# Nearest codes found in two steps: 256 folded pairs on VectorE with a clip on ScalarE, a choice inside the pair afterwards, and all 128 tiles of an image searched in one stage

## The chip, the cores and the metric

One core of a Trainium2 chip runs the whole kernel. The metric is the device time of one execution in microseconds (us), as the median of three runs. A profiled execution has a time of its own: the span from its first to its last instruction.

## What is computed

The input `x` is 8 images of 128 x 128 pixels with 32 channels. Two blocks follow each other, both added to what came in:

```python
x = x + conv_block(gn(x))       # Haar bands, nine small convolutions, attention, inverse Haar
x = x + vq(gn(x), codebook)     # codebook: 512 x 32
# vq, for every pixel:
dists = x_sq - 2.0 * (xf @ codebook.T) + c_sq
vq = codebook[argmin(dists)]
```

`gn` normalises each channel of an image over its pixels. The second line is what the change touches: for each of the 16384 pixels of an image the nearest of 512 codes is found, and that code is added to the pixel. The largest of `2 xf.c - |c|^2` is the smallest distance.

## The kernel before

**Stages.** `body(b, ...)` is run by every engine for b = 0 to 9. Stage b convolves image b (`conv`), searches codes for image v = b - 1 (`quant`), and loads and transposes image b + 1 (`nxt`). Stage 0 has no search, stage 7 loads nothing, stage 8 has the search of the last image and no convolution, and stage 9 only what stage 8 left over. All engines walk the same list `PLAN`, made by `make_plan` on the host, each issuing its own part at each step. So the order on every engine's queue is the order of `PLAN`, and each queue is in order.

**A stage's work on TensorE.** `PLAN` has 120 products in full float32 (`FULL`, two matmul records of 512 columns each) and 318 split terms (one record each). Between them are *turns*, which use the four PSUM banks `score`: 128 `tile` turns (one matmul of 128 pixels by 512 codes; `tile`, L886), 8 `ychunk` turns (four transposes of the image's pixels back to pixel-major order, copied to `ync` by `ycopy` on ScalarE), 8 `xchunk` turns (the same for the next image), and a few small ones: `mean2`, `var2`, `bias2` at the start of the stage and `mean1`, `var1` near its end. `spread_turns` decides between which products a turn goes. It keeps an account of VectorE's time (`ARGMAX` for a tile, `HAAR`, `PASS`) and places the next turn when that account is no more than `SHORT` = 1.17 or `LONG` = 1.38 us ahead of TensorE's. Turns take the banks round robin (`BANK`), so a turn needs the bank of the turn four places before it; `bank_free` is TensorE's wait for that.

**A tile.** TensorE scores it (L886). VectorE takes the eight largest of 512 scores (`maximum`, MAX8, L1499) and then finds the index (`index`, a load of the values and FIND_INDEX8, L1503); the index of tile t is issued behind the maximum of tile t + 1. The bank is free when the index is done (`s_idx`). GpSimd gathers the 128 code rows of 128 bytes by an indirect DMA into `vqc` (`gather`, L1618). After 16 tiles (a chunk) `add` on GpSimd adds the pixels in `ync` (L1632), and SyncE stores `vqc`.

**Late tiles.** `LATE` = 5: tiles 123 to 127 of an image are put off to the start of the following stage, between `mean2` and `bias2`, where the codes scaled for the following image don't exist yet.

**The stage's start.** `statistics`, `mean2`, `var2` on VectorE give the variance, GpSimd the root (`norm`), VectorE the scaled codes `cbs` (`scale_codes`), then `code_parts`, `bias2` and `bias_parts` on ScalarE and VectorE make `cst`, the table that every tile multiplies with. Tile 0 waits for it (`s_parts`).

**ScalarE's other work in its queue.** `evacuate` after each convolution (`z`, L1046), copies of edges behind some of them (`packed_copy`, L1034, six copies behind w12; `edge_copy`, L1023, two copies behind w25, w15, wd1 and wd2), `ycopy` (L1180), `xcopy` and `xorder` (L1169, L1163), `high` and `stack_high` (L1085, L1118: the left operand of the tiles, four casts after tiles 1 and 3 of every eight), `x_squares` (L1146, L1148), `restore`, `weighted_side`, `normal_ll`.

**A tie between two steps at the end of a stage.** `haar` 7 on VectorE follows tile 115, `x_squares(1)` on ScalarE waits for it, then come tiles 116 and 117, `mean1` on VectorE (which waits for the squares) and `var1` on TensorE (which waits for `mean1`).

## Time and profile before

| | |
|---|---|
| runs | 2001.28 us median, 2001.2 to 2004.69 |
| profiled execution, span | 1999.1 us |
| busy share of the span | TensorE 93%, VectorE 88%, GpSimd 63%, ScalarE 51% |
| one full stage | 225.0 us (the same pattern of steps at 708.95 and at 933.97) |
| end of the last convolution | about 1787.4 us |

The table of busy shares is an average over two very different parts: seven stages in which TensorE convolves one image while the others search the one before, and about 210 us at the end in which there is only the search of the last image. A stage's own windows must be read before a share says anything.

### The profile page before, as it was taken

What the parts mean: (1) busy time and instruction counts of PE and PEld (TensorE: products, weight loads), DVE (VectorE), ACT (ScalarE), POOL (GpSimd) and SP (SyncE); (2) the same over time, 40 slices, a digit from 0 to 9 for tenths busy, and PEclk for the clock granted to TensorE, in tenths of its full rate; (3) what the DMA queues carried; (4) which work ended last, traced back from release to release, by engine and by line L of the source; (5) the groups of instructions that cost most, each with busy time, mean ns of one, the idle gap of its engine ahead of it and who ended that gap; (6) DMA issues with size and microseconds to landing.
All of it is one profiled execution on the core that took longest, in us unless ns stands there. A gap on an engine that the chain in (4) does not pass through costs nothing.

```text
span 1999.1 us, 22686 instructions
## 1 busy us (share of the span) xinstructions
PE 1852.8 (93%) x6112; PEld 1114.6 (56%) x6112; DVE 1753.1 (88%) x3923; ACT 1025.9 (51%) x2058; POOL 1259.2 (63%) x1363
## 2 busy tenths in 40 slices
PE   7999999999999999999999999999999999985553
PEld 5654666456754666556754666556754666432221
DVE  5312799999999999999999999999999999989896
ACT  3325464746456464656456464656456453634331
POOL 1001267756777567766777567766677567767876
PEclk8999999999999999999999999999999999995555
DMA  6621463234532463234532463234532463201111
GB/s 190 186 79 48 111 154 99 71 92 117 157 80 69 116 156 104 71 84 128 156 82 70 116 155 104 72 85 128 154 83 54 112 154 90 60 19 34 37 37 32
DMA packets 135024, 197.21 MB, mean 99 GB/s; under 512 B 36977, under 2 KB 82545, under 8 KB 134897
## 3 DMA queue, kind: packets, MB, share of 16 engines
q1 hardware_dynamic: 101808, 178.40, 31.9%
q0 software_dynamic: 32768, 16.84, 5.4%
q8 instruction: 49, 0.80, 0.2%
q14 instruction: 79, 0.64, 0.1%
q10 hardware_dynamic: 320, 0.52, 0.1%
HBM read 117.52 MB, written 23.72 MB: 71 GB/s over the span
## 4 chain that ended last, share of the span: by engine, by line
PE 53%; DVE 29%; POOL 7%; ACT 5%; issue 5%; ACTq 0%; DMA 0%; POOLq 0%; DVEq 0%
PE ring L961 44%; DVE idx L1503 11%; DVE top L1499 10%; PE score L886 6%; POOL vqc L1618 5%; ACT yst L1118 2%; PE score L818 1%; DVE bands L1325 1%; ACT ha L1034 1%; POOL vqc L1632 1%; DVE brs L1388 1%; DVE ha L1388 1%; DVE bands L1443 1%; ACT hb L1034 1%; DVE bands L1439 1%
## 5 line engine op out<-in xcount | busy, mean ns | idle before, releaser
L1618 POOL DMA_INDIRECT vqc<-in_codebook,idx x1024 | 999.8, 976 | 447.9 <-DVE idx L1503 243.5
L1499 DVE MAX8 top<-score 128x8 f32<-128x512 f32 x1024 | 689.1, 683 | 50.1 <-PE score L886 31.3
L1503 DVE FIND_INDEX8 idx<-top,score 128x8 uint32<-128x512 f32 x1024 | 701.9, 689 | 0.0
L886 PE MATMUL score<-cst,yst 98*128 98x512 f32 x1024 | 619.7, 611 | 88.6 <-DVE idx L1503 70.6
L961 PE MATMUL ring<-hfp,wring 128*128 128x512 f32 x2160 | 594.1, 409 | 3.0 <-ACT hfp L1192 3.0
L961 PEld LDWEIGHTS ring<-hfp,wring 128*128 128x128 f32 x2160 | 409.1, 190 | 116.6 <-issue 10.8
L1118 ACT CAST yst<-bands 32x256 fp32r<-32x256 f32 x1024 | 411.7, 402 | 92.2 <-PE score L886 79.9
L961 PE MATMUL ring<-ha,wfull 128*128 128x512 f32 x896 | 439.1, 597 | 5.9 <-POOL ha L1650 5.2
L886 PEld LDWEIGHTS score<-cst,yst 98*128 98x128 f32 x1024 | 204.6, 202 | 293.8 <-DVE idx L1503 175.0
L961 PE MATMUL ring<-hb,wfull 128*128 128x512 f32 x736 | 356.6, 595 | 0.0
L961 PEld LDWEIGHTS ring<-ha,wfull 128*128 128x128 f32 x896 | 168.6, 190 | 150.3 <-issue 126.6
L961 PEld LDWEIGHTS ring<-hb,wfull 128*128 128x128 f32 x736 | 138.5, 189 | 128.3 <-issue 118.3
L1046 ACT ACTIVATE z<-ring,prm 128x512 f32<-128x512 f32 x144 | 98.9, 688 | 192.1 <-PE ring L961 188.0
L1180 ACT COPY ync<-score 128x256 f32<-128x256 f32 x128 | 41.4, 375 | 226.7 <-PE score L818 145.8
L1626 POOL TENSOR_TENSOR yl<-bands,yh 128x256 fp32r<-128x256 f32 x128 | 96.5, 757 | 15.8 <-ACT yh L1085 13.9
L1650 POOL TENSOR_TENSOR ha<-ha,brs 128x512 f32<-128x512 f32 x16 | 17.5, 1118 | 141.2 <-ACT brs L1063 141.0
L961 PE MATMUL ring<-sidep,wring 96*128 96x512 f32 x384 | 103.6, 405 | 0.0
L961 PE MATMUL ring<-pside,wfull 128*128 128x512 f32 x192 | 85.8, 595 | 0.0
L961 PEld LDWEIGHTS ring<-sidep,wring 96*128 96x128 f32 x384 | 72.5, 189 | 20.3
L1632 POOL TENSOR_TENSOR vqc<-vqc,ync 128x512 f32<-128x512 f32 x64 | 82.1, 1283 | 2.8 <-DMA vqc<-in_codebook,idx 1.7
L1606 POOL TENSOR_TENSOR rstd<-veps,power 128x1 f32<-128x1 f32 x16 | 17.4, 1090 | 104.0 <-DVE veps L1467 85.5
L1169 ACT COPY xt<-score 128x512 f32<-128x512 f32 x64 | 37.2, 583 | 80.2 <-PE score L818 57.1
(138 smaller groups left out, 1362.0 us busy)
## 6 DMA issues: line engine op xcount, KB each, us to landing
wring<-wparts SPq DMA_DIRECT2D x119, 384.0 KB, 3.4
hfp<-hfp SPq DMA_DIRECT2D x96, 255.0 KB, 5.1
yst<-yl SPq DMA_DIRECT2D x512, 32.0 KB
vqc<-in_codebook,idx POOLq DMA_INDIRECT x1024
out<-vqc SPq DMA_DIRECT2D x128, 128.0 KB
xnat<-in_x SPq DMA_DIRECT2D x112, 128.0 KB
wfull<-in_weights SPq DMA_DIRECT2D x32, 384.0 KB, 3.6
sidep<-hfp SPq DMA_DIRECT2D x96, 127.5 KB, 3.2
```

The costliest lines, as they stand in the source:

```text
L886: nc.tensor.matmul(score[bank][:, :], yst[0:KST, j % 2, g, wp], cst[0:KST, :], start=True, stop=True).then_inc(s_tile, 1)
L961: t = nc.tensor.matmul(ring[GBANK[key]][:, :, :], w[rows], src[rows], start=(i == first), stop=(i == last))
L1034: t = nc.scalar.copy(tiles[1][to * CH:(to + 1) * CH, dst, PAD:PAD + ROWS], tiles[0][group * CH:(group + 1) * CH, src, PAD + shift:PAD + sh ...
L1046: nc.scalar.activation(z[:, g % 2], bank[:, :, :], ACT.Identity, bias=col("b" + n[1:]))\
L1118: t = nc.scalar.copy(yst[part * CH:(part + 1) * CH, j % 2, g], block_of(par, j, slice(g * CH, (g + 1) * CH)))
L1180: t = nc.scalar.copy(dst[:, j], src[:, j])
L1388: nc.vector.scalar_tensor_tensor(out=dst, in0=z[:, g % 2], scalar=LEAK, in1=z[:, g % 2], op0=ALU.mult, op1=ALU.max).then_inc(s_leaky, 1)
L1499: nc.vector.max(top8[:, t % 4, :], score[bank][:, :]).then_inc(s_top, 1)
L1503: nc.vector.max_index(idx[:, t // CTILES % 2, t % CTILES, :], top8[:, t % 4, :], score[bank][:, :]).then_inc(s_idx, 1)
L1618: nc.gpsimd.indirect_dma_start(vqc[:, c % 2, w * CH:(w + 1) * CH], None, codebook[:, :], bass.IndirectOffsetOnAxis(idx[:, c % 2, k, 0:1], ...
L1626: nc.gpsimd.tensor_tensor(yl[:, j % 2], bands[par][:, :, j].rearrange("p w e i -> p w (e i)"), yh[:, j % 2], ALU.subtract).then_inc(s_yl, 1)
L1632: nc.gpsimd.tensor_tensor(vqc[:, c % 2, :], vqc[:, c % 2, :], ync[:, c % 2, :], ALU.add)\
```

## The change

What it does:

- **Pairs.** Code k and code k + 256 form a pair. The upper half of the score table holds the *difference* of the two codes, so the 512 columns of a tile's score are s(k) and s(k+256) - s(k). ScalarE clips the second half at zero (`rise`, Relu, 128 x 256, into `best`); VectorE adds the first half and takes the maximum in one instruction (`tensor_tensor_reduce`), then finds the index among 256. A bank is free after that first instruction (`s_top`), no longer after the index.
- **Inside the pair.** Rows of a table `pairs` in device memory hold both codes, their scaled difference and a threshold, 97 values (388 bytes). The scaled part is made once per stage: `table` on TensorE (two small matmuls), `table_rows` on ScalarE, two DMAs on SyncE. The gather fetches such a row. Every eight tiles `select` on VectorE runs four dependent instructions (multiply, reduce, compare, copy where upper), and `add` on GpSimd now covers eight tiles instead of sixteen.
- **Output.** The sum is written to `ync` and stored from there; `ycopy` waits for the store two chunks back instead of for `add`.
- **No late tiles.** `LATE` = 0; all 128 tiles lie in their own stage. `ARGMAX` is 1.2 instead of 1.286.
- **Space.** `pside` now lies over `sidep`, so SyncE's side copies wait for the last product of the stage before, and GpSimd writes the zero borders anew each stage (`rims`, `shore`).

```diff
-LATE = 5
+LATE = 0
-ARGMAX = 1.286
+ARGMAX = 1.2
...
+BOUNDARY = [("mean2", 6.9), ("var2", 9.3), ("scale2", 13.5), ("bias2", 16.9), ("table", 17.6)]
...
             def store(v, c):
-                sp.wait_ge(s_add, PRIMED + XCHUNKS * v + c + 1)
+                sp.wait_ge(s_add, HALVES * v + 2 * c + 2)
...
+            def table(v):
+                sp.wait_ge(s_tabs, v + 1)
+                wait(sp, s_add, HALVES * (v - 1))
+                for i in range(2):
+                    sp.dma_start(pairs[v % 2][i * P:(i + 1) * P, 2 * CH:ROW], tabs[:, i, :]).then_inc(s_table, 16)
...
                     if what == "tile" and 1 <= b <= IMAGES:
-                        return pe.wait_ge(s_idx, TILES * (b - 1) + k + 1)
+                        return pe.wait_ge(s_top, TILES * (b - 1) + k + 1)
...
+            def table_rows(v):
+                act.wait_ge(s_tabled, v + 1)
+                wait(act, s_table, 32 * v)
+                src = score[BANK["table",]][:, 0:2 * P].rearrange("p (i n) -> p i n", i=2)
+                nc.scalar.copy(tabs[:, :, :], src[:, :, 0:CH + 1]).then_inc(s_tabs, 1)
+
+            def rise(v, t, bank):
+                n = TILES * v + t
+                act.wait_ge(s_tile, n + 1)
+                wait(act, s_idx, n + 1 - SLOTS_R)
+                nc.scalar.activation(best[:, n % SLOTS_R, :], score[bank][:, PAIRS:CODES], ACT.Relu)\
+                    .then_inc(s_rise, 1)
...
             def ycopy(v, c):
                 act.wait_ge(s_yT, XCHUNKS * v + c + 1)
-                wait(act, s_add, PRIMED + XCHUNKS * v + c - 1)
+                wait(act, s_store[c % 2], 32 * ((XCHUNKS // 2) * v + c // 2))
...
             def maximum(v, t, bank):
-                wait(dve, s_tile, TILES * v + t + 1)
-                nc.vector.max(top8[:, t % 4, :], score[bank][:, :]).then_inc(s_top, 1)
+                dve.wait_ge(s_rise, n + 1)
+                nc.vector.tensor_tensor_reduce(
+                    out=best[:, n % SLOTS_R, :], in0=score[bank][:, 0:PAIRS], in1=best[:, n % SLOTS_R, :], scale=1.0,
+                    scalar=-ABSENT, op0=ALU.add, op1=ALU.max, accum_out=top8[:, t % 4, 0:1]).then_inc(s_top, 1)
...
+            def select(v, q):
+                n, c, h = HALVES * v + q, q // 2, q % 2
+                rows = picked[:, n % SLOTS_G, :].rearrange("p (t e) -> p t e", e=ROW)
+                y = ync[:, c % 2, h * JTILES * CH:(h + 1) * JTILES * CH].rearrange("p (t e) -> p t e", e=CH)
+                dve.wait_ge(s_yev, XCHUNKS * v + c + 1)
+                dve.wait_ge(s_gather[n % SLOTS_G], 128 * (n // SLOTS_G + 1))
+                after(nc.vector.tensor_tensor(prod[:, :, :], rows[:, :, 2 * CH:3 * CH], y, ALU.mult), s_lean, 3 * n + 1)
+                after(nc.vector.tensor_reduce(lean[:, 0, :], prod[:, :, :], AXIS.X, ALU.add), s_lean, 3 * n + 2)
+                after(nc.vector.tensor_tensor(lean[:, 1, :], lean[:, 0, :], rows[:, :, 3 * CH], ALU.is_gt),
+                      s_lean, 3 * n + 3)
+                upper = lean[:, 1, :].bitcast(U32).rearrange("p (t o) -> p t o", o=1).to_broadcast([P, JTILES, CH])
+                nc.vector.copy_predicated(rows[:, :, 0:CH], upper, rows[:, :, CH:2 * CH]).then_inc(s_select, 1)
...
                 nc.gpsimd.indirect_dma_start(
-                    vqc[:, c % 2, w * CH:(w + 1) * CH], None, codebook[:, :],
-                    bass.IndirectOffsetOnAxis(idx[:, c % 2, k, 0:1], 0)).then_inc(s_gather[c % 2], 16)
+                    picked[:, n % SLOTS_G, w * ROW:(w + 1) * ROW], None, pairs[v % 2][:, :],
+                    bass.IndirectOffsetOnAxis(idx[:, c % 2, k, 0:1], 0)).then_inc(s_gather[n % SLOTS_G], 16)
```

## Rows read from the trace of the kernel before

**Rows 1.** The page: busy time of the engines over the span

```profile
PE 1852.8 (93%) x6112; PEld 1114.6 (56%) x6112; DVE 1753.1 (88%) x3923; ACT 1025.9 (51%) x2058; POOL 1259.2 (63%) x1363
```

**Rows 2.** Busy time by window: one full stage, and the search alone

```profile
core 0: us, PE busy (x) PEld busy (x) DVE busy (x) ACT busy (x) POOL busy (x), PEclk, DMA share, GB/s
709.00:934.00 225.00, 221.69 (x762) 136.25 (x760) 217.37 (x487) 127.98 (x260) 156.91 (x165) 1.00 0.41 107
...
1809.00:1992.00 183.00, 99.73 (x156) 39.89 (x154) 163.55 (x385) 57.74 (x148) 141.96 (x151) 0.50 0.16 35
```

**Rows 3.** The chain of work, start and us: split terms, then full records

```profile
745.96 3.10 PE ring L961 x13
...
792.81 4.33 PE ring L961 x10
```

**Rows 4.** TensorE in order of time: the first tile of a stage, and its wait

```profile
909.58 0.60 PE L818 MATMUL score<-idn,bands 128*128 128x128 f32 x4
911.89 0.47 PE L886 MATMUL score<-cst,yst 98*128 98x512 f32 x1 [1.71 <-issue]
```

**Rows 5.** GpSimd in order of time: gathers in the search alone, an add

```profile
1872.99 1.28 POOL L1632 TENSOR_TENSOR vqc<-vqc,ync 128x512 f32<-128x512 f32 x1
1874.43 0.96 POOL L1618 DMA_INDIRECT vqc<-in_codebook,idx  x1 [0.16 <-issue]
...
1886.33 0.94 POOL L1618 DMA_INDIRECT vqc<-in_codebook,idx  x1 [0.31 <-issue]
1887.58 0.95 POOL L1618 DMA_INDIRECT vqc<-in_codebook,idx  x1 [0.30 <-issue]
...
1895.42 1.27 POOL L1632 TENSOR_TENSOR vqc<-vqc,ync 128x512 f32<-128x512 f32 x1
```

**Rows 6.** Groups by line and shape: count, busy us, mean ns, idle before

```profile
L1618 POOL DMA_INDIRECT vqc<-in_codebook,idx x1024 | 999.8, 976 | 447.9 <-DVE idx L1503 243.5 <-issue 195.4 <-DMA out<-vqc 7.8
L1503 DVE FIND_INDEX8 idx<-top,score 128x8 uint32<-128x512 f32 x1024 | 701.9, 689 | 0.0
L1499 DVE MAX8 top<-score 128x8 f32<-128x512 f32 x1024 | 689.1, 683 | 50.1 <-PE score L886 31.3 <-POOL vqc L1632 17.4
L1118 ACT CAST yst<-bands 32x256 fp32r<-32x256 f32 x1024 | 411.7, 402 | 92.2 <-PE score L886 79.9
L1180 ACT COPY ync<-score 128x256 f32<-128x256 f32 x128 | 41.4, 375 | 226.7 <-PE score L818 145.8 <-POOL vqc L1632 80.0
L1321 DVE TENSOR_TENSOR sd<-xt 128x256 f32<-128x256 f32 x56 | 23.4, 417 | 0.0
L1626 POOL TENSOR_TENSOR yl<-bands,yh 128x256 fp32r<-128x256 f32 x128 | 96.5, 757 | 15.8 <-ACT yh L1085 13.9
```

**Rows 7.** ScalarE in order of time: from the end of w12 on

```profile
708.36 0.69 ACT L1046 ACTIVATE z<-ring,prm 128x512 f32<-128x512 f32 x1 [0.76 <-PE ring L961]
708.95 4.05 ACT L1034 COPY ha<-ha 32x960 f32<-32x960 f32 x4
713.02 2.03 ACT L1034 COPY hb<-hb 32x960 f32<-32x960 f32 x2
715.08 0.65 ACT L1180 COPY ync<-score 128x256 f32<-128x256 f32 x2
```

**Rows 8.** TensorE in order of time: tile 19, the fourth turn behind the y transposes

```profile
715.77 0.50 PE L886 MATMUL score<-cst,yst 98*128 98x512 f32 x1
```

**Rows 9.** ScalarE in order of time: from the end of w25 to past wd1

```profile
801.35 0.69 ACT L1046 ACTIVATE z<-ring,prm 128x512 f32<-128x512 f32 x1 [4.05 <-PE ring L961]
804.03 2.03 ACT L1023 COPY hb<-hb 64x960 f32<-64x960 f32 x2 [1.99 <-DVE hb L1401]
...
815.89 2.03 ACT L1023 COPY ha<-ha 64x960 f32<-64x960 f32 x2 [1.18 <-DVE ha L1388]
...
819.62 3.30 ACT L1118 CAST yst<-bands 32x256 fp32r<-32x256 f32 x8
```

**Rows 10.** VectorE in order of time: the last step of mean1

```profile
876.10 0.22 DVE L1284 SCALAR_TENSOR_TENSOR vsum<-dev,vx 128x1 f32<-128x1 f32 x1
```

More of the change, by code:

```diff
@@ L10 @@
 U32 = mybir.dt.uint32
+AXIS = mybir.AxisListType
 P = 128
@@ L173 @@
 STARTS, SPREAD = bank_turns()
-TURNS = [x for x, _ in STARTS if x[0] not in ("var2", "scale2")] + SPREAD
+ORDERED = [x for x, _ in STARTS] + SPREAD
+TURNS = [x for x in ORDERED if x[0] not in ("var2", "scale2", "var1")]
 assert len(TURNS) % BANKS == 0
@@ L177 @@
 BANK["var2",] = BANK["mean2",]
+BANK["var1",] = BANK["mean1",]
 HAAR_AT = {c * CTILES + (XTURN if c < XCHUNKS - 1 else LASTX) + XDELAY - 1: c for c in range(XCHUNKS)}
-RUN_ENDS = [x[1] for x, y in zip(TURNS, TURNS[1:] + [("end",)]) if x[0] in ("tile", "late")
+RUN_ENDS = [x[1] for x, y in zip(ORDERED, ORDERED[1:] + [("end",)]) if x[0] in ("tile", "late")
             and (x[1] in (*HAAR_AT, NORMAL_AT, MAIN_TILES - 1, TILES - 1) or y[0] in ("mean1", "var1"))]
@@ L460, in conv_vq_kernel @@
         wparts = nc.dram_tensor("wparts", [P, NP * PAGE_SLOTS, P], F32, kind="Internal").ap()
+        pairs = [nc.dram_tensor(f"pairs{i}", [PAIRS, ROW], F32, kind="Internal").ap() for i in range(2)]
         at = (nc.sbuf_base + 31) // 32 * 32
@@ L710, in _ @@
                 sp.dma_start(dst[:, :], src[:, :]).then_inc(s_const, 16)
+            for rows in pairs:
+                for h in range(2):
+                    sp.dma_start(rows[:, h * CH:(h + 1) * CH], codebook[h * PAIRS:(h + 1) * PAIRS, :])\
+                        .then_inc(s_static, 16)
             def stack(v, j):
@@ L777, in body @@
                         stack(v, 1)
+                    elif quant and what == "table":
+                        table(v)
                     elif quant and what == "tile":
@@ L828, in bank_free @@
                         return pe.wait_ge(s_xev, XCHUNKS * (b + 1) + k + 1)
-                    if what in ("mean1", "var1") and b <= IMAGES - 2:
-                        return pe.wait_ge((s_dev if what == "mean1" else s_veps)[0], b + 2)
+                    if what == "mean1" and b <= IMAGES - 2:
+                        return pe.wait_ge(s_veps[0], b + 2)
                     if what == "ychunk" and 1 <= b <= IMAGES:
@@ L986, in body @@
                         bias2(v)
+                    elif quant and what == "table":
+                        bank_free(b, step)
+                        table(v)
                     elif quant and what == "ychunk":
@@ L1224, in body @@
                         bias_parts(v)
+                    elif quant and what == "table":
+                        table_rows(v)
+                    elif v > 0 and what == "late":
+                        rise(v - 1, step[1], BANK[step])
                     elif quant and what == "tile":
+                        rise(v, step[1], BANK[step])
                         j, k = step[1] // JTILES, step[1] % JTILES
@@ L1529, in body @@
                         pending = n, t, bank
+                        if t % JTILES == 4 and t > JTILES:
+                            select(n, t // JTILES - 1)
+                        if what == "tile" and t == 2 and n:
+                            select(n - 1, HALVES - 1)
                         if t in RUN_ENDS:
@@ L1673, in body @@
                             pending = None
-                        if t % CTILES == 11 and t > CTILES:
-                            add(n, t // CTILES - 1)
-                        if t == 3 and v:
-                            add(v - 1, XCHUNKS - 1)
+                        if t % JTILES == 6 and t > JTILES:
+                            add(n, t // JTILES - 1)
+                        if what == "tile" and t == 5 and n:
+                            add(n - 1, HALVES - 1)
                     elif nxt and what == "var1":
                         norm(0, b + 1)
+                    elif conv and what == "edge" and step[1] == 0:
+                        shore(b)
                     elif conv and what == "mm":
```

138 lines of the change are left out of this document (96 added, 42 removed).

## The prediction

> **What bounds the kernel now.** I read the busy table first, and distrust it: TensorE 93% and VectorE 88% [rows 1] look like two engines at their limit, and the change takes work from VectorE alone. The table by windows separates the parts. In a full stage of 225.0 us TensorE is busy 221.7 and VectorE 217.4 us, ScalarE only 128.0; in the search alone at the end TensorE's clock is at 0.50 (1.2 GHz, where it was at 1.00, or 2.4 GHz, in the stage), and VectorE and GpSimd share the time [rows 2].
>
> How much of the 225.0 us TensorE really needs is worked out from its own durations. Thirteen split terms took 3.10 us, so 0.2385 each; ten full records took 4.33 us, so a full product (two records) costs 0.87 us [rows 3]. A stage has 120 products (104.4 us), 318 terms (75.8), 128 tiles at 0.235 (30.1; the step from tile to next matmul in the stage, about one split term), 16 groups of transposes at 0.44 (7.0) and about 1.1 for the small ones: 218.4 us. So **TensorE stands idle 6.6 us per stage**, and that is all that a faster VectorE could give back there. Walking the program's order of turns with these costs and setting it against the times at which the tiles ran shows where it goes: about 3.2 us at the stage's start, where tile 0 waits for the code table (1.7 us of it as one wait [rows 4]), and 3.4 us in three places where VectorE or GpSimd was late.
>
> In the search alone the bound is neither TensorE nor VectorE. The gathers follow each other every 1.25 us (0.95 busy and 0.30 with nothing awaited), and from one add to the next 22.43 us pass for 16 tiles, with GpSimd nearly never waiting for an index [rows 5]. VectorE's pair of MAX8 and index steps every 1.26 us there (0.69 + 0.68 us overlapped, [rows 6]) but then stops for GpSimd.
>
> **VectorE's saving.** Before, 683 + 689 ns of searching per tile over 512 columns, in a step of 1.26 us [rows 6]. What 256 columns cost on VectorE has a row of another kind: a two-input pass of 128x256 takes 417 ns [rows 6], so I take 0.42 each for the sum with maximum and for the search, in all about 0.85 us per tile with the load of the values. The bounds are 0.75 (both halved in full) and 1.3 (nothing gained). `select` adds per eight tiles three passes of 256 elements and a tiny one with a semaphore between each: 3 x 0.42 + 0.15 + 0.15 = 1.5 us, 24 us per stage. VectorE's stage: 217 - 128 x 1.26 + 128 x 0.85 + 24 = 189 us (176 to 247). It stops being near the bound, unless nothing is gained per column. All this lies beside TensorE, so it brings at most the 3.4 us per stage.
>
> **What goes to ScalarE.** The clip reads 128x256 from PSUM as `ycopy` does: 375 ns, and two of those take 0.65 us [rows 6, 7]; I take 0.33 per tile, bounds 0.28 and 0.40. 128 of them are 42 us: ScalarE goes from 128 to 170 of 225 us, 76%. That sum looks harmless. But the clip is put into a queue in order, between a tile's matmul and the instruction that frees its bank. Before, a long block on ScalarE delayed the y and x copies alone; now it delays every tile behind it, and TensorE stops when four turns are outstanding. So each block is set against the turns that the changed plan places behind it:
>
> (a) *Behind w12.* From the start of w12's last evacuation to the end of the y copy behind six packed copies, 7.4 us pass (708.36 to 715.73) [rows 7]. In the plan before, the fourth turn behind the y transposes (tile 19) came 7.5 us after that product and ran at 715.77, just as its bank came free [rows 8]. In the changed plan the transposes come 1.7 us and tile 19 5.5 us after it: 1.9 us stall. Then ScalarE does clip, cast, clip, four casts (1.65 us, half of a 3.30 row [rows 9]) and clip before tile 18's bank is free: some 0.7 us more. 2.6 us.
>
> (b) *Behind w25, wd1 and wd2.* The evacuation of w25 starts, and 4.7 us later the edge copies are done (801.35 to 806.06), since ScalarE waits for VectorE in between; behind wd1 the edge copies and the squares together hold it from 815.89 to 819.62 [rows 9]. Behind each there is a y copy or `x_squares`, then tiles 0 to 3 of an eight with their four casts twice. Following the queue from w25's end on: tile 83 waits 0.15, tile 85 0.75, tile 92 0.95, tiles 100 and 101 0.85 each: 3.5 us.
>
> (c) *Behind haar 7.* `x_squares(1)` waits for VectorE's haar after tile 115. Before, tiles 116 and 117 were searched on VectorE while ScalarE squared. Now their clips wait behind the squares (1.7 us, from 817.92 to 819.62 [rows 9]), so `mean1`, which is behind their searches, ends some 8.6 us after tile 115's matmul. Before it was about the same (876.32 [rows 10], tile 115 at 867.9), but `var1` had a place 9.8 us after that matmul in the plan and now has one 6.3 us after it. 2.3 to 3.2 us, taken as 2.8.
>
> Sum 8.9 us of new stalls, against 3.4 us of old ones that go: **+5.5 us in a full stage**, 33 us in six. In stage 7 there is no next image, so (c) and the x copies are away; (a) and half of (b) remain, against 3.4: +1 us. Stage 0 has no search. Bounds: if ScalarE never makes TensorE wait the 3.4 us come back, -20 us over six stages; with 0.40 per clip and each stall half as long again it is +60.
>
> On exactly this the Trainium skill ("ScalarE: Activation LUTs", Rules for kernel authors) says for `relu`: use VectorE, not ScalarE. Here the clip as a pass on VectorE would cost another 0.42 by the row above, 54 us per stage, for 243 in 225; by that sum the rule doesn't fit a stage in which VectorE is at 217, yet what it warns of, ScalarE as the wrong place, is what my sum finds through the queue.
>
> **The stage's start.** The late tiles leave it: 5 x 0.235 = 1.2 us less TensorE work before tile 0 (they come back later in the stage, so nothing in sum), and VectorE is 2.5 us earlier with the scaled codes. But ScalarE is busy with eight casts until after that and then makes the table in a chain; tile 0 becomes possible about 1 us earlier, and TensorE arrives 1.1 us earlier. The 3.2 us stay. `table` adds two small matmuls (0.2 us; by the nearest rows between 0.06 and 0.9), a copy on ScalarE (0.35) and two DMAs on SyncE. Behind SyncE's wait for them are page loads, four pages ahead, which bear 2 us. Behind GpSimd's wait for the table is gather 0, some 1 to 2 us later. Zeroing of borders on GpSimd is ten short memsets, under 2 us, on an engine with slack in the stage (128 x 1.25 + 30 = 190 of 225). The side copies that now wait for the last product started just after it anyway. I cost these at nothing in the stage; cover gone would be 1 to 2 us.
>
> **The end.** GpSimd per 16 tiles: 16 x 1.25 = 20.0, two `low` passes at 0.61 more than the gap they fill (1.2), and the add: 1.15 more before, now two halves of 128x256. The row for that size on GpSimd is 757 ns [rows 6], so again 0.61 each beyond the gap, 1.2. 22.4 before, 22.5 after. The tiles that a faster VectorE delivers earlier find GpSimd at its own pace. The first gather comes about 0.7 us later, early waits for VectorE (some 4 us) mostly go, and at the very end stands `select` (+1.5) and a shorter add (-0.5). Sum for the end: -1 us, -4 to +3.
>
> **Sum.** 33 + 1 - 1 = +33 us on the profiled 1999.1 us, whose run lies as its span plus about 2.2 at the median of 2001.3: **2034 us**.
>
> **Rivals.**
> 1. *ScalarE keeps up.* Shares speak for it (76% busy), and the plan has gaps of 3 us behind each haar in which it catches up. Then TensorE's 3.4 us per stage come back: 2001.3 - 20 - 1 = 1980 us. Against it: block (a) passed before with no margin [rows 7, 8]. Chance 0.22, with a spread of 1975 to 1997.
> 2. *Both cancel*, stalls of 3.4 us per stage: 2001 us, within 4. Chance 0.08.
> 3. *The gather becomes dearer.* A row has 388 bytes instead of 128. If GpSimd needs 0.3 us more per gather (its unexplained 0.30 again), 128 x 1.55 + 30 = 228 us per stage make it the bound, and the end grows by 128 x 0.3 = 38 us: 2001 + 7 x 6 + 38 = 2081 us. It decides from about 0.25 us more per gather. For it: GpSimd alone sets the end [rows 5]. Against it: the number of rows per gather is unchanged at 128. Chance 0.08. The Trainium skill ("DMA: Bandwidth & Descriptors", Bandwidth) calls transfers below 64 KB descriptor-dominated, which would leave a gather of 50 KB near one of 16 KB.
> 4. *VectorE gains nothing*: the new pair costs 1.25 per tile, stage 217 + 24 = 241: 2001 + 7 x 16 + 15 = 2128 us. Chance 0.04.
>
> My forecast with its own range of 2005 to 2060 has 0.58: slower, at 2034. The range for 8 in 10 leaves out the far end of rival 1 and rivals 3 and 4: 1980 to 2058. Faster by over 0.2% (what a measurement of this kernel can tell from no change) 0.22, same 0.08, slower 0.70.
>
> **What would show it.** Steps right: stages of about 230.5 us; waits of TensorE's tiles and y/x turns for VectorE's new maximum or ScalarE's y copy, clustered behind w12, wd1, wd2 and before `var1`; ScalarE near 170 us busy per stage and VectorE near 190; gathers every 1.25 us and 22.5 us per 16 tiles at the end. Wrong: a stage of 221 to 222 us (rival 1), gathers further apart than 1.25 us in the end (rival 3), or a VectorE step per tile above 1.1 us (rival 4). The weakest step is (b), a queue followed over 40 us in which each delay shifts what comes behind it.

## The result: 213 us slower, and the profile after

The changed kernel takes 2214.7 us (median of four runs, 2214.0 to 2223.1), the kernel before 2001.2 us beside it: a ratio of 1.108, 95% interval 1.106 to 1.110. The forecast was slower, at 2034 us; the measured time lies far above its range. The profiled execution has a span of 2212.7 us. The experiments below are one execution each, so their times carry the scatter of single runs (the kernel before beside them: 1998.4 to 2002.2 us).

The page's line of busy times, which answers to [rows 1]:

```profile
PE 1920.9 (87%) x6144; PEld 1134.3 (51%) x6144; DVE 1422.7 (64%) x5465; ACT 1340.8 (61%) x3090; POOL 1283.7 (58%) x1483
```

The groups by line and shape that answer to [rows 6] (line, engine, operation, shapes, count, busy us, mean ns, idle time before them and what ended it):

```profile
L1725 POOL DMA_INDIRECT picked<-pairs,idx x1024 | 1002.7, 979 | 561.5 <-DVE idx L1579 360.4 <-issue 183.4 <-DMA pairs<-tabs 16.9
L1579 DVE FIND_INDEX8 idx<-top,best 128x8 uint32<-128x256 f32 x1024 | 424.9, 419 | 0.0
L1572 DVE CUSTOM_DVE_ANT_0 best<-score,best 128x256 f32<-128x256 f32 x1024 | 418.0, 415 | 469.5 <-ACT best L1175 467.1
L1175 ACT ACTIVATE best<-score 128x256 f32<-128x256 f32 x1024 | 365.6, 380 | 390.7 <-DVE idx L1579 284.6 <-PE score L931 100.9 <-issue 2.0
L1579 DVE MATCH_VALUE_LOAD idx<-top,best 128x8 f32 x1024 | 86.4, 84 | 1.7
L1572 DVE DVE_READ_ACCUMULATOR2_ANT top<- 128x1 f32 x1024 | 85.2, 83 | 0.0
L1589 DVE TENSOR_TENSOR prod<-picked,ync 128x256 f32<-128x256 f32 x128 | 55.8, 436 | 51.1 <-DMA picked<-pairs,idx 50.8
```

Every price was about as forecast: VectorE's fold 415 ns and its search 419 ns, the clip 380 ns, the gather 979 ns where it was 976 [rows 6]. VectorE is busy 330 us less than before [rows 1], and yet no engine is above 87%. The lines of the fold (L1572) and of the clip (L1175) say why: before each fold VectorE stood idle for ScalarE's clip, 467.1 us in all, and before each clip ScalarE stood idle for VectorE's index, 284.6 us. Each of the two engines waits for the other (e3 below tells what the second of these waits is worth).

Busy time by window (us, then each engine's busy time, the granted clock, the DMA share, GB/s), for one full stage from `mean2` to `mean2` and for the search alone at the end, against [rows 2]:

```profile
734.33:990.25 255.92, 231.96 (x765) 138.28 (x764) 175.74 (x679) 166.77 (x387) 160.23 (x180) 0.97 0.43 111
1999.00:2212.00 213.00, 100.63 (x171) 44.02 (x170) 137.41 (x599) 107.56 (x296) 147.41 (x162) 0.51 0.23 51
```

This stage takes 255.9 us where it took 225.0. The last convolution ends at 1999.3 us (before at 1787.4, of a span of 1999.1), so the search alone behind it takes 213.4 us, 1.6 more than before. Everything else, some 212 us, came in the stages: 194 in the six full ones (from tile 0 to tile 0, 32 each) and 18 in stage 7.

### The profile page after: what moved, and what is told of

Read it like the earlier page. It is cut to its first block, busy times and chain, and to the rows that moved or that the text cites. A ratio compares the mean times of both kernels' runs of the same rounds, so it can differ in the third digit from the quotient of the medians.

```text
span 2212.7 us, 26665 instructions
## 1 busy us (share of the span) xinstructions
PE 1920.9 (87%) x6144; PEld 1134.3 (51%) x6144; DVE 1422.7 (64%) x5465; ACT 1340.8 (61%) x3090; POOL 1283.7 (58%) x1483
## 4 chain that ended last, share of the span: by engine, by line
PE 34%; DVE 24%; ACT 15%; issue 12%; DMA 8%; SPq 4%; POOL 3%; ACTq 0%; DVEq 0%; POOLq 0%
PE ring L1008 30%; DVE idx L1579 6%; ACT yst L1185 6%; DVE best L1572 4%; DMA xnat<-in_x 4%; DMA picked<-pairs,idx 4%; ACT best L1175 3%; PE score L931 3%; POOL picked L1725 2%; DVE picked L1594 2%; DVE lean L1590 2%; DVE prod L1589 2%; DVE ha L1461 1%; SPq L754 1%; SPq L777 1%
## 5 line engine op out<-in xcount | busy, mean ns | idle before, releaser
L1725 POOL DMA_INDIRECT picked<-pairs,idx x1024 | 1002.7, 979 | 561.5 <-DVE idx L1579 360.4
L1572 DVE CUSTOM_DVE_ANT_0 best<-score,best 128x256 f32<-128x256 f32 x1024 | 418.0, 415 | 469.5 <-ACT best L1175 467.1
L1175 ACT ACTIVATE best<-score 128x256 f32<-128x256 f32 x1024 | 365.6, 380 | 390.7 <-DVE idx L1579 284.6
L1008 PE MATMUL ring<-ha,wfull 128*128 128x512 f32 x896 | 461.8, 622 | 29.9 <-DVE ha L1461 29.3
L1579 DVE FIND_INDEX8 idx<-top,best 128x8 uint32<-128x256 f32 x1024 | 424.9, 419 | 0.0
L1008 PE MATMUL ring<-hb,wfull 128*128 128x512 f32 x736 | 368.1, 615 | 9.1 <-DVE hb L1474 5.7
L1742 POOL TENSOR_TENSOR ync<-ync,picked 128x256 f32<-128x256 f32 x128 | 101.1, 790 | 5.6 <-DVE picked L1594 3.3
L1589 DVE TENSOR_TENSOR prod<-picked,ync 128x256 f32<-128x256 f32 x128 | 55.8, 436 | 51.1 <-DMA picked<-pairs,idx 50.8
L1579 DVE MATCH_VALUE_LOAD idx<-top,best 128x8 f32 x1024 | 86.4, 84 | 1.7
L1572 DVE DVE_READ_ACCUMULATOR2_ANT top<- 128x1 f32 x1024 | 85.2, 83 | 0.0
```

The costliest lines, as they stand in the source:

```text
L1008: t = nc.tensor.matmul(ring[GBANK[key]][:, :, :], w[rows], src[rows], start=(i == first), stop=(i == last))
L1175: nc.scalar.activation(best[:, n % SLOTS_R, :], score[bank][:, PAIRS:CODES], ACT.Relu)\
L1572: nc.vector.tensor_tensor_reduce(out=best[:, n % SLOTS_R, :], in0=score[bank][:, 0:PAIRS], in1=best[:, n % SLOTS_R, :], scale=1.0, scalar= ...
L1579: nc.vector.max_index(idx[:, t // CTILES % 2, t % CTILES, :], top8[:, t % 4, :], best[:, n % SLOTS_R, :]).then_inc(s_idx, 1)
L1589: after(nc.vector.tensor_tensor(prod[:, :, :], rows[:, :, 2 * CH:3 * CH], y, ALU.mult), s_lean, 3 * n + 1)
L1725: nc.gpsimd.indirect_dma_start(picked[:, n % SLOTS_G, w * ROW:(w + 1) * ROW], None, pairs[v % 2][:, :], bass.IndirectOffsetOnAxis(idx[:, c ...
```

## Where a stage loses its time

As for the forecast, I set the tiles' times against the program's order of turns. TensorE loses 37.5 us per stage to waits and to a lower clock behind them, where it lost 6.6. By place: the stage's start 2.8; behind w12 3.0; tiles 30 to 74 6.3; tiles 80 to 101 (w25, wd1, wd2) 13.2; from `mean1` to tile 121 9.2; in pieces under 0.6 us 3.0.

The largest single piece is at wd2's start. The changed kernel in order of time (start, us, operation, idle time before it and its releaser), first TensorE:

```profile
890.18 1.02 PE L1008 MATMUL ring<-hb,wfull 128*128 128x512 f32 x2
895.72 2.05 PE L1008 MATMUL ring<-ha,wfull 128*128 128x512 f32 x2 [4.51 <-DVE ha L1461]
```

ScalarE in the same stretch:

```profile
888.35 0.71 ACT L1230 COPY xord<-xnat 128x256 f32<-128x256 f32 x2 [1.26 <-DMA xnat<-in_x]
888.96 0.65 ACT L1175 ACTIVATE best<-score 128x256 f32<-128x256 f32 x2
889.50 0.69 ACT L1096 ACTIVATE z<-ring,prm 128x512 f32<-128x512 f32 x1
890.30 0.38 ACT L1175 ACTIVATE best<-score 128x256 f32<-128x256 f32 x1
892.50 0.38 ACT L1175 ACTIVATE best<-score 128x256 f32<-128x256 f32 x1 [1.81 <-DVE idx L1579]
892.78 0.68 ACT L1096 ACTIVATE z<-ring,prm 128x512 f32<-128x512 f32 x1
897.70 2.02 ACT L1073 COPY ha<-ha 64x960 f32<-64x960 f32 x2 [4.23 <-DVE ha L1461]
```

And VectorE:

```profile
889.37 0.42 DVE L1572 CUSTOM_DVE_ANT_0 best<-score,best 128x256 f32<-128x256 f32 x1 [3.21 <-ACT best L1175]
...
890.13 0.40 DVE L1589 TENSOR_TENSOR prod<-picked,ync 128x256 f32<-128x256 f32 x1
...
891.23 0.47 DVE L1594 COPY_PREDICATED picked<-lean,picked 128x256 f32<-128x256 uint32 x1
...
892.91 0.41 DVE L1393 TENSOR_TENSOR sd<-xt 128x256 f32<-128x256 f32 x1
...
894.36 1.21 DVE L1461 SCALAR_TENSOR_TENSOR ha<-z 128x512 f32<-128x512 f32 x1
```

Read it as one story. ScalarE waits 1.26 us for an x transfer that has nothing to do with the search. Behind that copy stand two clips, so VectorE stands for 3.21 us, though the haar's input behind its fold had been ready since 887.08 (`xt`, copied by ScalarE). When the clip comes, VectorE does fold, index, `select` (890.13 to 891.70), a fold and two searches, a haar (892.9 to 894.4) and only then the leaky step of wd1, whose input z had been ready at 890.2: 4.2 us late. TensorE, which needs that `ha`, stands 4.51 us. Meanwhile ScalarE stands 1.81 us for an index three tiles back and then 4.23 us for the second half of that `ha`, which VectorE makes behind two more folds and two searches (896.99 to 897.67). Behind ScalarE's edge copies and the squares of `x` the next clips wait: VectorE stands again, 4.15 us before its fold at 901.81. A delay on either queue is handed to the other and comes back.

Before, VectorE's searches waited only for TensorE (31.3 us in all) and for GpSimd (17.4) [rows 6]; none of them waited for ScalarE.

## The experiments

Two parts of the diff stand apart in most of them: the clip, and ARGMAX 1.2, which places tiles, y transposes, `mean1` and `var1` closer (1.286 is the constant of the kernel before).

**e1, no clip on ScalarE.**

```diff
-                        rise(v, step[1], BANK[step])
...
-                dve.wait_ge(s_rise, n + 1)
+                dve.wait_ge(s_tile, n + 1)
+                wait(dve, s_idx, n + 1 - SLOTS_R)
                 nc.vector.tensor_tensor_reduce(
-                    out=best[:, n % SLOTS_R, :], in0=score[bank][:, 0:PAIRS], in1=best[:, n % SLOTS_R, :], scale=1.0,
+                    out=best[:, n % SLOTS_R, :], in0=score[bank][:, 0:PAIRS], in1=cb4[:, 0:PAIRS], scale=1.0,
```

> The kernel after without the clip on ScalarE: the first pass of VectorE adds a constant table from SBUF instead of the clipped second half, so the choice of code is not the reference's. ScalarE is out of the tile's path, all else (select, table, gathers of 388 bytes, spacing) stays. Theory (the clip's place in ScalarE's queue, between the matmul and the instruction that frees the bank, makes the time): stages fall from 255.9 to 220 to 228 us, time 1975 to 2025 us. Rival 1 (select and the gathers it waits for on VectorE make the time): stages stay above 240, time above 2110. Rival 2 (the new spacing with all 128 tiles in one stage makes it): stages stay above 240 as well.

2077.7 us: 137 us come back, but 76 more than before remain, 53 above the expected band. So the clip's place in the queue is the largest part, and something that I had costed at nothing makes up the rest. A stage took 234.6 us, with TensorE's losses spread: start 2.8, tile 19 2.2, tile 64 1.7, tile 83 1.3, `mean1` 1.6, `var1` 2.5, tiles 119 to 121 2.6.

**e2, ScalarE as busy, but nobody waits.** VectorE folds as in e1.

```diff
-SLOTS_G, SLOTS_R = 3, 3
+SLOTS_G, SLOTS_R = 2, 3
...
-                wait(act, s_idx, n + 1 - SLOTS_R)
-                nc.scalar.activation(best[:, n % SLOTS_R, :], score[bank][:, PAIRS:CODES], ACT.Relu)\
-                    .then_inc(s_rise, 1)
+                wait(act, s_rise, n)
+                nc.scalar.activation(spare[:, :], cb4[:, 0:PAIRS], ACT.Relu).then_inc(s_rise, 1)
```

> As the run without the clip, but ScalarE runs a Relu of 128x256 per tile at the clip's place on data in SBUF, after the tile's matmul; nobody waits for it (the choice of code is not the reference's; two gather slots instead of three make room). If ScalarE's occupied time alone delays its evacuations: 2080 to 2200 us. If it is the wait of VectorE and of the bank for the clip that costs: within 25 us of the run without the clip.

2113.7 us, 36 above e1 and 101 below the changed kernel: in the first band, and 11 above the second. The stand-in reads SBUF and takes 417 ns where the clip takes 380, so it fills 53 us of ScalarE's time per stage and the clip 46. That time costs some 36 us in the whole run; what is left of the clip, above all that VectorE and the bank wait for it, costs the other 101. The two gather slots are a second difference between these kernels; in e11 below they come with six slots for the clip and cost nothing.

**e3, six slots in place of three**, so that ScalarE may clip further ahead:

```diff
-SLOTS_G, SLOTS_R = 3, 3
+SLOTS_G, SLOTS_R = 2, 6
```

> Complete kernel, six buffers for the clipped scores instead of three (two gather slots instead of three), so ScalarE never waits for VectorE's index of three tiles before. In the profile after, ScalarE idles 285 us on that wait. Theory that this wait closes a circle (VectorE stops in select or haar, ScalarE stops for it, and y copies and evacuations queue behind): 2100 to 2170 us. If the wait is only where ScalarE would have been idle anyway: within 15 us of 2214.

2191.7 us, 23 less, outside both bands. ScalarE's wait for the index is gone (2.8 us in all, before the edit 284.6), but it then waits for TensorE's tile:

```profile
L1175 ACT ACTIVATE best<-score 128x256 f32<-128x256 f32 x1024 | 361.8, 381 | 301.3 <-PE score L931 294.5 <-DVE idx L1579 2.8 <-issue 1.1
```

VectorE still stands 430.4 us for the clip, where it stood 467.1. So the distance of three tiles is a small part: a late clip is late however far it was allowed ahead. If delays come back to ScalarE at a high price, then by its other waits for VectorE, those of the edge copies and squares for the leaky and haar steps. That way was seen in the rows above; no run took it out.

**e4, `select` left out:**

```diff
-                after(nc.vector.tensor_tensor(prod[:, :, :], rows[:, :, 2 * CH:3 * CH], y, ALU.mult), s_lean, 3 * n + 1)
...
-                nc.vector.copy_predicated(rows[:, :, 0:CH], upper, rows[:, :, CH:2 * CH]).then_inc(s_select, 1)
+                nc.vector.memset(lean[:, 0, :], 0.0).then_inc(s_select, 1)
```

> The kernel after with the four instructions of select left out (the wait for the gathers and for the y copy stays, a small memset signals; the lower code of every pair is always taken). Theory of the clip's place: VectorE is not the bound, 10 to 60 us less than 2214. Rival (select is the cause): below 2100.

2139.5 us, 75 less: more than the 10 to 60 that I gave it, though not the rival's 115. The forecast had put `select` on VectorE as 24 us a stage "beside TensorE". It was not beside: the four instructions stood between late clips and late leaky steps. `select`'s wait for the gathers stays in this kernel (89.7 us of VectorE's idle time), so the 75 us are the price of the four instructions alone.

**e5 to e7, the spacing.** The first line is e5; e6 adds e1's edit; e7 adds the others to e5, the clip as a pass on VectorE with none on ScalarE:

```diff
-ARGMAX = 1.2
+ARGMAX = 1.286
...
+                dve.wait_ge(s_tile, n + 1)
+                nc.vector.tensor_scalar_max(best[:, n % SLOTS_R, :], score[bank][:, PAIRS:CODES], 0.0).then_inc(s_rise, 1)
                 dve.wait_ge(s_rise, n + 1)
```

> Complete kernel after with ARGMAX = 1.286 as before, so the turns lie further apart again (tile 19 comes 7.9 us behind w12's last product instead of 5.7, var1 9.8 us behind tile 115 instead of 6.3). Theory (the spacing is a cause of its own beside the clip): 2140 to 2185 us. If only the clip's place counts: within 15 us of 2214.

> ARGMAX = 1.286 and no clip on ScalarE (VectorE adds a constant table, the choice of code is not the reference's). The run without the clip took 2078 us with the tight spacing; its idle time of TensorE sat at tile 19, at mean1 and var1 and at tiles 64 and 83. Theory: tile 19, mean1 and var1 pass again, 2010 to 2045 us. Rival (select and its gathers make the rest): above 2060 us.

> Complete kernel, ARGMAX = 1.286, the clip as a pass of its own on VectorE (128x256, 0.42 us, 54 us per stage on top of some 171 busy). Theory (the place of the clip costs more than its length): faster than the same spacing with the clip on ScalarE, 2070 to 2140 us. If VectorE's length decides: over 2180 us.

2142.3, 2014.6 and 2131.3 us, all as expected. The spacing is worth 72 us with the clip and 63 without it: the two parts nearly add. In the plan for 1.2 the first y transposes behind w12 come 1.7 us after its end and `var1` some 6.3 us after tile 115; in that for 1.286 it is 4.0 and 9.8 us, by the forecast's prices. The clip on VectorE, as the Trainium skill ("ScalarE: Activation LUTs", Rules for kernel authors) has it for `relu`, is 11 us better than on ScalarE here. The runs agree with that rule, though by little, and both lie 130 to 141 us above the kernel before: a third pass per tile costs on either engine.

**e8, e11, e12: two mends, together and apart.** e11 gives e5 the slots of e3. e12 moves `select` and the add one tile later, so that the gathers' transfers have landed. e8 does both:

```diff
-                        if t % JTILES == 4 and t > JTILES:
+                        if t % JTILES == 5 and t > JTILES:
                             select(n, t // JTILES - 1)
...
-                        if t % JTILES == 6 and t > JTILES:
+                        if t % JTILES == 7 and t > JTILES:
                             add(n, t // JTILES - 1)
```

> Complete kernel with the clip on ScalarE, ARGMAX = 1.286, six buffers for the clipped scores (two gather slots), and select and add one tile later each. Theory: the parts add up, 2100 to 2160 us; still slower than before, since evacuations stay behind the clips in ScalarE's queue.

> ARGMAX 1.286 with SLOTS_G, SLOTS_R = 2, 6 (complete kernel): ScalarE may clip six tiles ahead of VectorE's index in place of three, and the gathers have two slots in place of three. Beside the next run this tells which of e8's two edits made it 27 us slower than e5 (2142.3). At ARGMAX 1.2 the same edit gained 23 us: if it gains here too 2115 to 2135; if two gather slots are too few at this spacing, over 2150 with GpSimd's adds late and TensorE's clock lower than e5's 0.935.

> ARGMAX 1.286 with select one tile later (fifth tile of an eight in place of the fourth) and the add one tile later. Expected if select's wait for the gathers' transfers is what holds VectorE: 2125 to 2140. If it is this edit that cost e8 its 27 us: 2150 to 2175, since the y copy behind it then waits for the store of a later add.

2169.2, 2141.8 and 2184.5 us, in the order e8, e11, e12: all three outside their bands. At this spacing the slots do nothing beside the early `select` (e11 against e5) and gain 15 us beside the late one (e8 against e12). The later `select` costs 42 us, though its wait for the gathers fell (0.8 us between 700 and 956 us of the trace, in e5 1.6). I expected a gain for e8, and it was 27 us worse than e5.

The traces show where: over the six full stages e12 loses 50 us between tiles 102 and 115 and e5 13, and in five of them 4.55 us go before tile 106 alone. GpSimd there adds `brs` to `ha` and to `hb`, two sums at a time. e12, GpSimd:

```profile
918.19 2.15 POOL L1771 TENSOR_TENSOR ha<-ha,brs 128x512 f32<-128x512 f32 x2
...
923.50 2.15 POOL L1771 TENSOR_TENSOR hb<-hb,brs 128x512 f32<-128x512 f32 x2
```

VectorE, and TensorE behind it:

```profile
918.21 2.42 DVE L1589 TENSOR_TENSOR prod<-picked,ync 128x256 f32<-128x256 f32 x1
...
923.05 2.90 DVE L1397 TENSOR_TENSOR bands<-sd 128x256 f32<-128x256 f32 x1
```

```profile
926.68 0.50 PE L931 MATMUL score<-cst,yst 98*128 98x512 f32 x1 [3.98 <-DVE top L1572]
```

`select`'s multiply and a haar pass, usually 0.4 us each, took 2.42 and 2.90, and each ended 0.3 us behind GpSimd's pair. In e5 one haar pass stands beside the first pair (1.69 us), and beside the second only folds and searches, which took no longer than usual. So one tile later puts two of VectorE's passes beside GpSimd's sums instead of one. That the sums hold VectorE is read from the times; no run moved them.

**e9, TensorE kept busy in two of its waits.** The windows around wd2's start (columns as above) show the granted clock beside TensorE's idle time:

```profile
885.00:890.00 5.00, 4.94 (x13) 2.42 (x14) 1.78 (x12) 3.68 (x10) 2.93 (x4) 1.00 0.48 137
890.00:895.00 5.00, 1.21 (x4) 0.33 (x2) 4.86 (x17) 1.53 (x4) 2.94 (x4) 0.82 0.19 46
895.00:900.00 5.00, 4.28 (x6) 2.16 (x7) 2.66 (x10) 2.27 (x3) 3.02 (x3) 0.50 0.39 81
900.00:905.00 5.00, 5.00 (x15) 2.60 (x15) 2.09 (x11) 4.93 (x15) 1.00 (x2) 1.00 0.07 19
```

TensorE was busy 1.21 of 5 us, and the clock fell from 1.00 (2.4 GHz) to 0.50 (1.2 GHz) until 900 us. The step of a product with its tile was 2.27 and 2.09 us behind the wait, 1.10 before it. The kernel before has no such stretch: from 250 us to its last convolution the clock is at 1.00 in every window of 2.5 us. Over the stages (250 us to the last convolution) TensorE is busy 1587 us here and 1512 before, and some 48 of these 75 us are the lower clock (busy time in windows of 2.5 us, times one less the clock). That looked like a cause of its own, so e9 fills two waits with matmuls that nothing reads:

```diff
+            def fill(dst, times):
+                for _ in range(times):
+                    nc.tensor.matmul(dst, cst[0:KST, 0:P], cst[0:KST, CODES - dst.shape[-1]:CODES], start=True, stop=True)
...
+                    if b > 0 and (n, half) == ("wd2", 0) and i == first:
+                        for _ in range(17):
+                            nc.tensor.matmul(ring[GBANK[key]][:, :, :], cst[0:KST, 0:P], cst[0:KST, :],
+                                             start=True, stop=True)
                     inputs_ready(b, n, half, m, kind, low)
...
                         bank_free(b, step)
+                        if quant:
+                            fill(score[BANK[step]][:, PAIRS:CODES], 20)
                         mean(0, b + 1, BANK[step])
```

> The changed kernel with matmuls that nothing reads, put in front of two of TensorE's long waits: 20 of 98x128 by 98x256 before mean1's (its wait was 2.85 us), 17 of 98x128 by 98x512 into wd2's own bank before its first input (4.51 us); the next start=True overwrites them. TensorE waits as long but isn't idle. In the changed kernel's trace the granted clock was at 0.50 behind these two places (895 to 900 and 950 to 956 us) and at 1.00 ahead of them, and never below 1.00 in a stage of the kernel before. Theory 'the idle time costs twice, once as a wait and once as half the clock behind it': the clock stays at 1.00 behind wd2's start and mean1, and since a product with its tile took 2.1 us there and 1.09 at full clock, 2.2 us and up to 3 us a stage come back: 2214.7 less 15 to 35 us, 2180 to 2200. Rival 'TensorE would wait for VectorE there anyway, so its clock is free': within 6 us of 2214.7, at a clock of 1.00 or not. Slower by more than 6 us if the fillers run on beyond the wait.

2223.1 us: not 15 to 35 less, but 8 more, as long as the slowest of the changed kernel's own four runs. TensorE of e9 in order of time:

```profile
892.85 4.43 PE L1010 MATMUL ring<-cst 98*128 98x512 f32 x17
898.45 1.13 PE L1017 MATMUL ring<-ha,wfull 128*128 128x512 f32 x2 [1.17 <-DVE ha L1472]
...
905.12 0.50 PE L936 MATMUL score<-cst,yst 98*128 98x512 f32 x1 [1.15 <-DVE top L1583]
```

And the window of e9 behind the fillers:

```profile
897.50:902.50 5.00, 4.05 (x12) 2.19 (x12) 2.98 (x10) 1.97 (x2) 3.31 (x4) 1.00 0.34 72
```

At wd2's start the edit did what it should: the clock stayed at 1.00 and the step was 1.1 to 1.2 us. But TensorE then met VectorE's fold 1.15 us too early, and from the product behind the wait to `mean1` it took 52.55 us (898.45 to 951.00), in the changed kernel 52.53 (895.72 to 948.25). What the clock gave was handed back as waits: there the lower clock is a symptom, and the pace is set by VectorE and ScalarE. At `mean1` the edit worked by half: its wait fell from 2.85 to 0.37 us, but `var1` then waited 3.79 us where it had waited 2.39, and behind it the clock fell all the same (0.52 from 955 to 960 us). The fillers ran on beyond neither wait (1.17 and 0.37 us of idle time behind them). By the sum above 31 us of lower clock were left of the 48.

**e10, e2's edit at 1.286.**

> ARGMAX 1.286, and ScalarE does its clip on other data in SBUF that nobody waits for (VectorE folds with a constant, so the second half of the scores is left out of the search): the queue is as long, the handshake is gone. At this spacing the clip with its handshake cost 128 us (2142.3 against 2014.6). Theory 'the handshake is the larger part': 2030 to 2060. Rival 'ScalarE's queue is the larger part': over 2080. At ARGMAX 1.2 the occupancy alone was worth 36 us.

2052.0 us, as expected: 37 above e6 and 90 below e5. ScalarE's time costs the same at both spacings (36 and 37), and the wait nearly so (101 and 90).

**e13, e14, e17: the length of ScalarE's blocks.** From the second image on the edge copies move one column:

```diff
+                width[0] = 1 if b else ROWS
...
-                    t = nc.scalar.copy(tiles[1][p, dst, PAD:PAD + ROWS], tiles[0][p, src, PAD:PAD + ROWS])
+                    t = nc.scalar.copy(tiles[1][p, dst, PAD:PAD + width[0]], tiles[0][p, src, PAD:PAD + width[0]])
```

(and so for line 1084), in the changed kernel (e13), in the kernel before (e14), and in e1 (e17).

> The changed kernel, but from the second image on the 14 edge copies of a stage on ScalarE (lines 1073 and 1084, 1.00 us each) move one column in place of 64, so the edges are old ones; their waits for VectorE and their signals stay. About 12 us of ScalarE's 167 go, all of it out of the long blocks that the prediction named in (a) and (b). Theory 'it is the blocks': behind them the clips come late, and most of the 101 us that the clip's handshake costs (2214.7 against e2's 2113.7) goes with them: 2110 to 2155. Rival 'it is the handshake at every tile, and the waits of the blocks, not their copies': 2180 to 2210.

> The control: the same edit in the kernel before (lines 1023 and 1034 there; from the second image on the edges are old ones). TensorE stands idle some 3.4 us a stage there outside the stage's start, and the copies lie ahead of a few x and y turns: 1985 to 2001. A gain of more than 20 us would mean that e13's gain is not the clip's.

> e13's edit without the clip: ARGMAX 1.2, no clip on ScalarE (the second half of the scores is left out of the search), and the edge copies of one column from the second image on (old edges). With the clip the short copies gained 66 us, in the kernel before 14. Theory 'their length matters through the clip's queue': 2055 to 2070 against e1's 2077.7. Rival 'they gain as much at this spacing without the clip': 2010 to 2030.

2148.6, 1986.5 and 2047.1 us: 66, 14 and 31 us less, the first two as expected. The same microseconds of ScalarE cost nearly five times as much with the change as before. Without the clip half of the gain is left (e17 missed both bands, in the middle). What makes the copies count twice as much as before even there, the closer places or something else of the change, wasn't tried apart.

**e15, e16: `select` with and without the clip, at 1.286.**

> ARGMAX 1.286 and select's four instructions left out (a memset in their place, so the lower code of each pair is always taken). At ARGMAX 1.2 select cost 75 us, of which 24 a stage of VectorE's time were not on any path by the prediction. Theory 'select holds VectorE's queue, and the clip's handshake passes that on whatever the spacing': 2060 to 2090. Rival 'select mattered at 1.2 because the tiles came too close': 2115 to 2140.

> e15's edit without the clip: ARGMAX 1.286, no clip on ScalarE (VectorE folds with a constant, so the second half of the scores is left out of the search), and select's four instructions left out. With the clip select cost 60 us at this spacing (2142.3 against 2082.3). Theory 'the handshake makes VectorE's queue a part of TensorE's way': without it select costs little, 1998 to 2010 against e6's 2014.6. Rival 'select costs the same by itself': 1950 to 1975, which would lie below what TensorE needs.

2082.3 and 1997.1 us (the latter 1 us below its band). Without `select` the time falls by 60 us with the clip, by 17.5 without it. This shows the coupling most plainly: VectorE's queue matters three times as much once the clip ties ScalarE to it. Both kernels keep `select`'s wait for the gathers, 104 us of VectorE's idle time in e16, which is as fast as the kernel before: that wait is no part of the loss.

Put in a row, each step is one measured difference:

| kernel | us | step |
|---|---|---|
| before, beside e16 | 1998.4 | |
| e16: all but clip, `select` and spacing | 1997.1 | -1 |
| e6: with `select` | 2014.6 | +17 |
| e10: with the clip's time on ScalarE | 2052.0 | +37 |
| e5: with the wait for the clip | 2142.3 | +90 |
| the change: with ARGMAX 1.2 | 2214.7 | +72 |

e10's two gather slots are inside its two steps. Another order of the steps would give other sizes, since they act on each other (`select` is 17 us without the clip and 60 with it). No version here beats the kernel before: only the incomplete e14 and e16 lie below it.

## Why the prediction was right and where it failed

*Right.* The direction. VectorE's price: I took 0.85 us per tile; two folds followed each other at 884.58 and 885.33, so 0.75, the lower bound. The clip's 0.33 (two took 0.63 us), ScalarE's 170 us per stage (166.8), `select`'s 1.5 us (1.57). The gather's price, and with it the end:

```profile
2120.74 0.69 POOL L1742 TENSOR_TENSOR ync<-ync,picked 128x256 f32<-128x256 f32 x1
...
2124.11 0.94 POOL L1725 DMA_INDIRECT picked<-pairs,idx  x1 [0.30 <-issue]
...
2143.16 0.69 POOL L1742 TENSOR_TENSOR ync<-ync,picked 128x256 f32<-128x256 f32 x1
```

Two adds stand 22.42 us apart over 16 tiles, forecast 22.5, and the end came out at +1.6 us, forecast -1 within -4 to +3. Rivals 3 and 4 are out by their own rows, rivals 1 and 2 by the time. GpSimd issues three times the bytes in the same time. For the transfers themselves the Trainium skill ("DMA: Bandwidth & Descriptors", Bandwidth), which calls those below 64 KB descriptor-dominated, holds only in part here. The gathers' queue on the page (packets, MB, share of the 16 engines' time), first before, then after:

```profile
q0 software_dynamic: 32768, 16.84, 5.4%
```

```profile
q0 software_dynamic: 32768, 50.92, 10.8%
```

With as many packets and three times the bytes they take 2.2 times as long, 117 ns a packet where it was 53, by these shares of the two spans. That stays away from the end, where GpSimd's issuing sets the pace.

The stage's start: 2.8 us, forecast 3.2. And block (a), the one whose rows of before held everything: ScalarE went from 770.37 to 777.73 (7.36 us, forecast 7.4), and tile 19 stood for it. ScalarE:

```profile
770.37 0.69 ACT L1096 ACTIVATE z<-ring,prm 128x512 f32<-128x512 f32 x1 [0.22 <-DVE ha L1461]
...
777.08 0.65 ACT L1247 COPY ync<-score 128x256 f32<-128x256 f32 x2
```

TensorE's tiles 19 and 21:

```profile
777.77 0.50 PE L931 MATMUL score<-cst,yst 98*128 98x512 f32 x1 [2.31 <-ACT ync L1247]
...
780.88 0.50 PE L931 MATMUL score<-cst,yst 98*128 98x512 f32 x1 [0.19 <-DVE top L1572]
```

3.0 us by the walk through the plan, forecast 2.6.

*Wrong: step (b), 13.2 us for 3.5.* I followed ScalarE's queue and let VectorE always be on time. The rows at 888 to 898 us show what was left out: once VectorE waits for the clip, its leaky and haar steps are late too; ScalarE's edge copies wait for those, and the clips behind them wait again. My durations were right there, but each was added once, where the two queues pass a delay to and fro. [rows 9] should have warned me, since it holds waits of ScalarE for VectorE of 1.99 and 1.18 us: waits of the kind that close the circle. wd2's start itself, where 4.51 us went in one wait, wasn't on my list at all.

*Wrong: step (c), 9.2 us for 2.8.* TensorE of the changed kernel:

```profile
948.25 0.56 PE L895 MATMUL score<-mv,gmean 128*128 128x1 f32 x2 [2.85 <-DVE mv L1404]
...
953.54 0.56 PE L895 MATMUL score<-vsum,gmean 128*128 128x1 f32 x2 [2.39 <-DVE vsum L1357]
```

I had counted `var1` alone; `mean1` waits 2.85 us too, and 2.5 of these come neither from the circle nor from `var1`'s place. I took haar 7's length as it was before. Its second pass, first before, then in the changed kernel:

```profile
870.73 0.42 DVE L1321 TENSOR_TENSOR sd<-xt 128x256 f32<-128x256 f32 x1
```

```profile
943.68 2.90 DVE L1394 TENSOR_TENSOR sd<-xt 128x256 f32<-128x256 f32 x1
```

And GpSimd beside the latter:

```profile
944.14 2.14 POOL L1771 TENSOR_TENSOR hb<-hb,brs 128x512 f32<-128x512 f32 x2
```

These are the sums that hold VectorE in e12. Before, a haar pass was held like this in five of the six full stages, but in haar 6 (849.21 to 852.12). The changed kernel has it in haar 7 in all six, right ahead of what `mean1` and the squares need, and so has e1; e5, at 1.286, has it in haar 6. The rest of (c) is `var1`'s wait and the lower clock behind both (0.53 and 0.50 from 947.5 to 957.5 us).

*Wrong: the stretch of tiles 30 to 74, 6.3 us for nothing.* There was no block in my list there, but there are clips, casts, `select` and y copies; which of them it is wasn't told apart.

*Wrong: stage 7, 18 us for 1*, for which I had (a) and half of (b).

*Wrong: `select` "beside TensorE".* It cost 17 us even without the clip (e16 to e6), and 60 to 75 with it. VectorE has 80 idle us in a stage of 256, and they hide nothing if the instruction stands ahead of one that TensorE needs.

*Wrong: the spacing taken as a matter of (a) and (c).* ARGMAX 1.2 alone is 63 to 72 us, 9 to 10 a stage. A tile placed too early doesn't run early: TensorE, in order, waits in front of it with all products behind.

*The bound.* My upper bound, +60 us, was "each stall half as long again". With a queue whose waits depend on another queue that is not a bound; the runs show a factor of nearly four on (b).

## What to carry to other kernels

Before an operation is put between two engines that both work in order, draw the waits in both directions: if the receiver's queue holds anything that the giver waits for, the price is not its busy time but every delay of either queue passed on to the other, here 37 us for the time and 90 for the wait. Test an added step by its effect on what stands behind it in the queue, not by the engine's share. And before a plan's constants are tightened for one faster engine, look at what else the places hang on: they were set by VectorE's new speed, and even without the clip the closer ones cost 63 us (e1 against e6), with stops at tile 19, whose bank waits for ScalarE's y copy, and at `mean1` and `var1`. The price of a pass is not a constant either: look which engine works beside it.

## What the runs showed of the hardware

- TensorE's granted clock fell to 0.50 in the middle of a stage after it had been busy 1.21 of 5 us; the matmuls went on at 895.72, and from 900 us the clock was at 1.00 (windows above). Keeping it at 1.00 there by fillers gained nothing (e9, +8 us): TensorE wasn't the pace.
- A VectorE pass with two inputs took 2.90 us in place of 0.42 beside two sums of GpSimd's of 128x512, and ended 0.3 us behind them (943.68 to 946.58; in e12 also `select`'s multiply, 2.42 us).
- Gathers of 128 rows cost GpSimd 979 ns each with rows of 388 bytes and 976 ns with 128 bytes; their packets took 117 and 53 ns each.
